# A language-model block on one core: the first layer's bias as a weight row, one of eight weight rows subtracted from the rest, two experts' low parts made by VectorE, and new orders on four engines

## The reference, cut to what matters

```python
# x is the layer-normalised hidden row: 4096 tokens x 64
gate_logits = x_flat @ Wg + bg + bias                       # 8 logits
topk_vals, topk_idx = jax.lax.top_k(gate_logits, 2)
topk_w = jax.nn.softmax(topk_vals, axis=-1)
h = jax.nn.relu(jnp.einsum('td,edh->teh', x_flat, W1) + b1) # 8 experts, 64 -> 128
y = jnp.einsum('teh,ehd->ted', h, W2) + b2                  # 128 -> 64
out = jnp.einsum('ted,te->td', y, combine)
```

## Time and profile before

| | us |
|---|---|
| median of 3 runs | 90.46 (89.78 to 91.33) |
| the profiled execution | 90.22 |
| its span, from the first to the last instruction | 88.4 |
| PE busy in the span | 76.5 (87%) |
| DVE busy | 73.0 (83%) |
| ACT busy | 69.1 (78%) |
| POOL busy | 57.2 (65%) |

### The profile page before, as it was taken

One profiled execution on the slowest core, in us unless ns is written; L12 is line 12 of the kernel. 1 busy time (PEld: TensorE's weight loads), 2 busy tenths in 40 slices (PEclk: granted clock), 3 DMA queues, 4 the chain that ended last, 5 costly groups with the idle time before them and its releaser, 6 DMA issues.

```text
span 88.4 us, 2799 instructions
## 1 busy us (share of the span) xinstructions
PE 76.5 (87%) x1004; PEld 48.7 (55%) x1004; DVE 73.0 (83%) x305; ACT 69.1 (78%) x141; POOL 57.2 (65%) x111
## 2 busy tenths in 40 slices
PE   0098899779869999999999999999999999999920
PEld 0055794444346676556556676654754557667900
DVE  5899989999994999699978999998995599349970
ACT  0579995428147998999999999999999987996530
POOL 7030009898718848599534889989897788983420
PEclk9999999995899999999999999999999999999998
...
GB/s 20 110 151 261 389 56 4 0 0 8 0 0 0 7 0 0 7 1 4 0 7 0 0 7 0 0 7 0 0 52 8 7 4 51 15 0 0 64 163 137
DMA packets 5919, 3.40 MB, mean 39 GB/s; under 512 B 4914, under 2 KB 5266, under 8 KB 5906
## 3 DMA queue, kind: packets, MB, share of 16 engines
...
q10 hardware_dynamic: 512, 0.31, 1.2%
...
...
## 4 chain that ended last, share of the span: by engine, by line
PE 47%; DVE 22%; ACT 14%; POOL 9%; issue 5%; POOLq 0%; ACTq 0%
PE bank L1344 12%; PE bank L1371 6%; PE bank L1353 6%; PE bank L1173 6%; ACT hid_lo L691 4%; PE bank L1368 3%; PE bank L1374 3%; ACT oneh_junk L631 2%; ACT hid_hi L684 2%; ACT ids_all L603 2%; POOL h_part L457 2%; PE bank L1257 2%; DVE prod_pair L1012 1%; DVE pT L925 1%; PE bank L1402 1%
## 5 line engine op out<-in xcount | busy, mean ns | idle before, releaser
L684 ACT ACTIVATE hid_hi<-bank,b_down 128x512 f16<-128x512 f32 (+1 forms) x40 | 26.5, 663 | 2.9 <-PE bank L1344 2.4
L691 ACT ACTIVATE hid_lo<-bank,b_col 128x512 f16<-128x512 f32 (+1 forms) x40 | 26.6, 664 | 0.1
L1353 PE MATMUL bank<-hid_hi,minus_h 128*128 128x512 f16 (+1 forms) x40 | 14.4, 361 | 0.2
L1344 PE MATMUL bank<-xT,w_hi 128*128 128x512 f16 (+1 forms) x40 | 14.4, 359 | 0.1
L1344 PE MATMUL bank<-xT,w_lo 128*128 128x512 f16 (+1 forms) x40 | 14.3, 357 | 0.0
L1006 DVE TENSOR_TENSOR prod<-bank,comb 128x512 f32<-128x512 f32 x14 | 9.4, 690 | 4.8 <-PE bank L1374 4.6
L559 POOL TENSOR_TENSOR half<-prod 128x256 f32<-128x256 f32 x12 | 8.8, 733 | 1.2 <-DVE prod L1006 0.4
L1173 PE MATMUL bank<-toe_hi,oneh_j 128*128 128x512 f16 (+3 forms) x24 | 9.0, 378 | 0.0
L1353 PEld LDWEIGHTS bank<-hid_hi,minus_h 128*128 128x128 f16 x40 | 3.9, 97 | 8.5 <-ACT hid_hi L684 6.6
L1173 PE MATMUL bank<-toe_lo,oneh_j 128*128 128x512 f16 (+3 forms) x24 | 8.5, 375 | 0.0
L1371 PE MATMUL bank<-w_lo,hid_hi 128*128 128x64 f16 x112 | 8.4, 193 | 0.0
...
## 6 DMA issues: line engine op xcount, KB each, us to landing
w_sb<-in_w1g_dram SPq DMA_DIRECT2D x1, 516.0 KB, 5.2
...
w_sb<-in_w2b_dram SPq DMA_DIRECT2D x1, 260.0 KB, 5.4
...
```

Of the source, the lines that this page charges most:

```text
L684: act.activation(hid_hi[:, k % 2, e, 0:m], bank[n % LBANKS][:, 0:m], ACT.Relu, bias=b1_down[:, e:e + 1], scale=KEEP * HSCALE / (XSCALE * X ...
L691: act.activation(hid_lo[:, k % 2, e, 0:m], bank[n % LBANKS][:, 0:m], ACT.Relu, bias=b1_col[:, e:e + 1], scale=HSCALE / (XSCALE * XSCALE)). ...
L1344: ins = mm(bank[n % LBANKS][:, 0:m], w[:, HID * e:HID * (e + 1)], xT[:, k % 2, 0:m], start=part == 0, stop=part == 1)
L1353: mm(bank[n % LBANKS][:, 0:m], minus_h[:], hid_hi[:, k % 2, e, 0:m], start=False, stop=True, skip_group_check=True).then_inc(s_rest, 1)
```

## The change

1. The first layer's bias becomes a row of its weights. The 64 entries of x sum to zero, so entry 63 is minus the sum of the others: the kernel subtracts weight row 63 from rows 0 to 62 (`w1_centre` on POOL, a 128x1032 subtraction, with a new 516 KB load `w63` ahead of `w2` on SP), and puts the bias into row 63. DVE sets entry 63 of x to a constant once (`bias_column`), and `rows_c` writes 63 entries of 64.
2. ACT no longer adds a bias in `high` and `low`, the scales become powers of two, and the two small activations that prepared the bias are gone. `w1_high` waits for `w1_centre`.
3. For experts 2 and 6 of every unit, PE's `take_high` and ACT's `low` are gone, and DVE writes `hid_lo` in one instruction: max(bank, 0) - `hid_hi` (`hidden_low`). These are ten of the forty. What waited for `s_hid` now waits for one of two semaphores.
4. The lists of calls of POOL, ACT, DVE and PE are new.

```diff
@@ the load (SP)
             sp.dma_start(w1_sb[:], w1g).then_inc(loads["w1"], 16)
-            sp.dma_start(w2_sb[:], w2b1).then_inc(loads["w2"], 16)
+            sp.dma_start(w63_sb[:], w63).then_inc(loads["w63"], 16)
+            sp.dma_start(w2_sb[:], w2).then_inc(loads["w2"], 16)
             sp.dma_start(b2_row[:], b2).then_inc(loads["b2"], 16)
@@ POOL
+            def w1_centre():
+                pool.wait_ge(loads["w1"], 16)
+                pool.wait_ge(loads["w63"], 16)
+                pool.tensor_tensor(w1_sb[:], w1_sb[:], w63_sb[:], ALU.subtract).then_inc(s_w1c, 1)
...
-            rsqrt_hidden(); table_values(); embed_parts(); skip_values(); rsqrt1(0); value_parts(); rsqrt2(0)
+            rsqrt_hidden(); bias_parts(); embed_parts(); w1_centre(); table_values(); skip_values(); rsqrt1(0)
...
@@ ACT
             def w1_high():
-                act.wait_ge(loads["w2"], 16)
-                act.mul(b1_col[:], w2_sb[:, EXPERTS * D:], HSCALE)
-                act.mul(b1_down[:], w2_sb[:, EXPERTS * D:], HSCALE * KEEP)
-                act.wait_ge(loads["w1"], 16)
-                act.mul(w1_hi[:], w1_sb[:], XSCALE).then_inc(s_w1h, 1)
+                act.wait_ge(s_w1c, 1)
+                act.mul(w1_hi[:], w1_sb[:], WS).then_inc(s_w1h, 1)
...
@@ DVE
+            def hidden_low(n):
+                k, e = n // EXPERTS, n % EXPERTS
+                m = P * SIZE[k]
+                dve.wait_ge(s_high, n + 1)
+                dve.scalar_tensor_tensor(hid_lo[:, k % 2, e, 0:m], bank[n % LBANKS][:, 0:m], 0.0, hid_hi[:, k % 2, e, 0:m],
+                                         ALU.max, ALU.subtract).then_inc(s_hidv, 1)
...
@@ PE, first_layer
                 else:
-                    pe_.wait_ge(s_hid, n + 1 - LBANKS)
+                    wait_expert(pe_, n - LBANKS)
...
-                if n:
+                if n and (n - 1) % EXPERTS not in DVE_LOW:
                     take_high(n - 1)
...
-            turn_ids(); spread_ids(0); spread_ids(1); spread_ids(2); spread_ids(3); turn_top(); fold_weights()
+            spread_ids(0); spread_ids(1); turn_ids(); spread_ids(2); spread_ids(3); turn_top(); fold_weights()
...
-            weights(0); turn_exps(); attend(0, 2); scores(0); scores(1); embed(0); weights(1); scores(2); attend(2, 4)
...
+            embed(0); weights(0); turn_exps(); scores(0); attend(0, 2); scores(1); weights(1); scores(2); embed(1)
...
```

More of the change, by code:

```diff
@@ L79, with build @@
 QW = C_PROJ + D + 2
-def build(nc, x, token_w, vecs, qkv, bias_table, w1g, w2b1, b2, out):
+def build(nc, x, token_w, vecs, qkv, bias_table, w1g, w63, w2, b2, out):
     ids_dram = nc.dram_tensor("ids_scratch", (SEQS, LEN), BF16, kind="Internal").ap()
@@ L370, in build, with by_dve, by_act, wait_expert @@
         LOGITS = bank[5][:, 448:448 + MAXB * EXPERTS]
+        DVE_LOW = (2, 6)
+        def by_dve(n):
+            return sum(i % EXPERTS in DVE_LOW for i in range(n))
+        def by_act(n):
+            return n - by_dve(n)
+        def wait_expert(eng, n):
+            if n % EXPERTS in DVE_LOW:
+                eng.wait_ge(s_hidv, by_dve(n + 1))
+            else:
+                eng.wait_ge(s_hid, by_act(n + 1))
         class Chain:
@@ L733, in _ @@
+            hidden(4, 1); choice_exp(4); hidden(4, 2); hidden(4, 3); hidden(4, 4); hidden(4, 5); hidden(4, 6)
+            hidden(4, 7); low(4, 7); read_look(0); read_look(1); read_look(2)
         @block.vector
@@ L1073, in _ @@
-            rows_b(0); rows_b2(0); part_low(0); rows_c(0); toeplitz_low(1); rows_d(0); skip_exps(); rows_a(1)
-            rows_b(1); rows_b2(1); key_part(1); choose_a(0); rows_c(1); key_part(2); rows_d(1); skip_key()
-            skip_key_rows(); choose_b(0); rows_a(2); choose_a(1); rows_b(2); rows_b2(2); choose_b(1); rows_c(2)
-            key_part(3); rows_a(3); rows_d(2); rows_b(3); rows_b2(3); weigh(0); weigh(1); choose_a(2); weigh(2)
-            rows_c(3); rows_a(4); choose_b(2); rows_d(3); weigh(3); rows_b(4); rows_b2(4); weigh(4); weigh(5)
@@ new lines, in _ @@
+            skip_masks(); skip_columns(); penalties(); values(); row_maxima(); split_exps(); toeplitz_low(1)
+            flat_weights(); w1_low(); rows_a(0); key_part(0); rows_b(0); rows_b2(0); part_low(0); rows_c(0)
+            key_part(1); rows_d(0); rows_a(1); skip_exps(); early_one_hots(); rows_b(1); rows_b2(1); skip_key()
+            rows_c(1); skip_key_rows(); choose_a(0); rows_d(1); hidden_low(2); key_part(2); choose_b(0); rows_a(2)
+            choose_a(1); rows_b(2); hidden_low(6); key_part(3); rows_b2(2); choose_b(1); rows_c(2); rows_a(3)
@@ new lines, in _ @@
+            hidden_low(10); rows_d(2); weigh(0); rows_b(3); rows_b2(3); weigh(1); hidden_low(14); choose_a(2)
+            rows_a(4); choose_b(2); weigh(2); rows_c(3); hidden_low(18); rows_b(4); weigh(3); rows_d(3); rows_b2(4)
+            hidden_low(22); weigh(4); weigh(5); rows_c(4); choose_a(3); rows_d(4); weigh(6); hidden_low(26)
+            choose_b(3); weigh(7); weigh(8); hidden_low(30); weigh(9); choose_a(4); weigh(10); choose_b(4)
+            hidden_low(34); weigh(11); weigh(12); weigh_pair(0); weigh(13); hidden_low(38); gather_two(); weigh_pair(1)
@@ L1435, in _ @@
-            turn(0); weights(2, 0, 1); weights(2, 1, 3); first_layer(0, 0); weights(2, 3, 4); embed(1)
-            first_layer(0, 1); scores(3); first_layer(0, 2); weights(2, 4, 5); first_layer(0, 3); skip_weights()
-            gate(0); weights(2, 5, 8); first_layer(0, 4); skip_scores(); first_layer(0, 5); weights(3, 0, 1)
-            weights(3, 1, 3); first_layer(0, 6); weights(3, 3, 5); turn(1); first_layer(0, 7); skip_turn()
-            attend(6, 4); first_layer(1, 0); gate(1); first_layer(1, 1); embed(2); first_layer(1, 2); weights(3, 5, 8)
@@ L1450, in _ @@
-            last_bias(3); last_bias(4); look_up(0); take_high(EXPERTS * UNITS - 1); last_layer(4); last_layer(5)
-            last_layer(6); last_layer(7); look_up(1); look_up(2)
+            embed(0); weights(0); turn_exps(); scores(0); attend(0, 2); scores(1); weights(1); scores(2); embed(1)
+            weights(2, 0, 1); attend(2, 4); weights(2, 1, 3); turn(0); weights(3, 0, 1); weights(3, 1, 3)
+            first_layer(0, 0); scores(3); weights(2, 3, 4); weights(2, 4, 5); first_layer(0, 1); gate(0)
@@ new lines, in _ @@
+            skip_weights(); skip_scores(); first_layer(0, 2); weights(2, 5, 8); first_layer(0, 3); skip_turn()
+            weights(3, 3, 5); weights(3, 5, 8); first_layer(0, 4); turn(1); attend(6, 4); first_layer(0, 5); gate(1)
+            first_layer(0, 6); first_layer(0, 7); embed(2); first_layer(1, 0); first_layer(1, 1); embed(3)
+            first_layer(1, 2); first_layer(1, 3); attend(10, 4); first_layer(1, 4); second_layer(0); first_layer(1, 5)
+            turn(2); first_layer(1, 6); first_layer(1, 7); second_layer(1); gate(2); embed(4); first_layer(2, 0)
@@ new lines, in _ @@
+            attend(14, 4); first_layer(2, 1); second_layer(2); first_layer(2, 2); first_layer(2, 3); second_layer(3)
+            first_layer(2, 4); first_layer(2, 5); second_layer(4); first_layer(2, 6); first_layer(2, 7); turn(3)
+            second_layer(5); first_layer(3, 0); last_bias(0); gate(3); first_layer(3, 1); second_layer(6)
+            first_layer(3, 2); second_layer(7); first_layer(3, 3); turn(4); first_layer(3, 4); first_layer(3, 5)
+            second_layer(8); first_layer(3, 6); first_layer(3, 7); second_layer(9); first_layer(4, 0); gate(4)
```

110 lines of the change are left out of this document (54 added, 56 removed).

## The result

Before 90.70 us (median of 4 runs, 89.78 to 91.33), after 94.69 (4 runs, 93.93 to 94.85): ratio 1.046, 95% interval 1.035 to 1.057. The change makes the kernel slower by some 4 us, by a late start, as forecast (93.6 was predicted). The profiled execution took 94.57, its span 92.8, against 90.22 and 88.4 before.

The account below looks back on a forecast made before the run. ACT was the tighter bound before; DVE's queue bounds afterwards. Start 24.4 plus 60.6 work plus 0.6 waits ends gather_two at 85.6 instead of 82.19, +3.4 on 90.22: 93.6 us, range 90.9 to 96.2.

Parts of the forecast that it names:

- b2's landing: At the start, b2 lands behind w63 and w2 at 12.2 us, between 10.2 and 13.6; POOL's bias_parts waits for it.
- Rival B: Start less late: b2 lands 1.4 us sooner, embed_parts is 1.2 shorter; no change, 91.0 us in all; chance 0.20.
- POOL agrees: At the start, POOL's queue behind w1_centre frees rsqrt1(0) at about 24.4 us, matching rows_a(0).
- the port: Shared SBUF port at the start: DVE's moved toe_lo holds POOL up to 0.7 us more, making the result 94.3.
- hid_lo on DVE: Ten new DVE instructions in the experts' stretch, 0.60 to 0.69 us each at full width, 5.7 us taken together.
- DVE's work in the stretch: From rows_a(0) to the end of gather_two, DVE has 54.2 + 5.7 + 1.3 - 0.6 = 60.6 us of work.
- rival C: Relief of ACT and PE pays and DVE's stretched operations shrink: faster, 86.4 or 88.5 us; chance 0.07.
- New waits: DVE's waits between rows_a(0) and the end of gather_two: 0.6 us, between 0 and the old 7.8.
- those for PE go: DVE's old waits for PE, 1.82 and 1.27 us, vanish because DVE itself is now later.
- the bias costs the same either way: On ACT, dropping the bias and changing the scales saves no time.
- The check on PE: first_layer(1, 1) on PE waits for hidden_low(6) on DVE; costs only where DVE has to wait in turn.
- rival D: DVE and PE wait for each other over banks holding low parts: 3 us more, 96.6 us; chance 0.11.

Follow-up runs that it names:

- experiment 8: experiment 1 with gather(10) and gather(11) ahead of the fin_parts on POOL, and look_up(0) behind last_layer(7) on PE: 94.22 us, ratio 1.038.
- 11: Changed kernel with b2 loaded first, w1_centre on DVE, the start orders of before, and gather(10) ahead of the fin_parts: 96.79 us, ratio 1.063.
- 4: Changed kernel with all forty low parts on PE and ACT, none on DVE: 96.44 us, ratio 1.068.
- 5: experiment 1 with all forty low parts on PE and ACT, none on DVE: 95.28 us, ratio 1.049.
- experiment 1: Changed kernel with the b2 load issued first, ahead of SP's wait for the ids: 92.59 us, ratio 1.025.
- 9: experiment 1 with the start of ACT, PE and DVE (up to toeplitz_low(0)) in the order of the kernel before: 92.98 us, ratio 1.022.
- experiment 7: Kernel before plus one 128x1032 POOL subtraction, into a tile nobody reads, where POOL was idle: 92.34 us, ratio 1.016.
- 6: experiment 1 with the w1_centre subtraction moved from POOL to DVE, behind toeplitz_low(0): 92.59 us, ratio 1.020.
- experiment 12: Changed kernel with b2 first, w1_centre on DVE, old start orders, embed(0) behind scores(1), attend(0) and squares(0) moved earlier: 93.43 us, ratio 1.028.

## Why the prediction was right

Right: the sign, and that the loss is a late start, made by POOL's queue behind `b2`. The sum's total was 1.0 us short (93.6 against 94.57 profiled; 94.69 in the median), within its own range: `gather_two` ended 0.5 later than predicted (86.10, not 85.6), and the end behind it, which I had left as it was, grew by 0.4. That it came so near is in part luck, since two pairs of errors cancelled. Step by step:

- **b2's landing**: predicted 12.2, at most 13.6; measured 13.4. `w63` added 1.3 us, as predicted (issued at 5.66, 6.0 to landing: 11.66, against `w1`'s 10.38). Most of the missing 1.2 is `w2`'s: it landed at 13.2, 1.6 behind `w63`, not 0.7; the loads were also issued 0.2 later. Rival B's other case, a small load overtaking, is refuted here: 2 KB issued at 6.61 came last. The Trainium skill (DMA: Bandwidth & Descriptors, "Queues, rings and completion order") allows an overtaking; this trace shows none.
- **bias_parts**: 2.0 predicted, 2.0 measured. **embed_parts**: 4.4 predicted, 3.0 measured, just under its lower end of 3.2: `w_lo`, beside which its first cast had taken 1.44, no longer ran beside it. **w1_centre**: 2.3 and 2.44. The errors cancel, which is luck, and `w_sb` is ready at 20.93, predicted 20.9 to 21.2.
- **rows_a(0)**: 24.4 and 24.48. But "POOL agrees", with `rsqrt1(0)` free at 24.4, was 1.1 too early: it started at 25.48, and DVE waited 0.43 for it (see the port, below).
- **hid_lo on DVE**: 0.60 to 0.69 predicted, 0.60 in a row and 0.69 alone measured; the ten are 6.3 us busy in records that overlap their neighbours by some 0.08 each, against 5.7 predicted in steps. No mistake there.
- **DVE's work in the stretch**: 60.6 predicted. Measured: 61.62 less 4.6 of waits behind the first mark, 57.0. This step was wrong by 3.6 us. Part of it is that `gate_bias` left the stretch (0.3 in steps), which I overlooked, and part that some of DVE's short operations shrank, which I had put under rival C only. POOL is 1.3 us less busy in the stretch; that this is the reason isn't shown. Two of them, from the groups of this stretch, the kernel before first:

```profile
L999 DVE TENSOR_TENSOR comb<-sel 128x32 f32<-128x32 f32 (+1 forms) x5 | 1.6, 319 | 0.2
```

```profile
L1029 DVE TENSOR_TENSOR comb<-sel 128x32 f32<-128x32 f32 (+1 forms) x5 | 1.2, 245 | 0.2
```

   Of the busy time, groups of this kind shrank by 2.0 us together (`gw`, `comb`, `xn`, `gd`, `var`), while `gs`, `xs` and `og` grew by 0.6. The rest of the 3.6 I can't place.
- **New waits**: 0.6 predicted, 4.6 measured ("under 2 us" was among my own signs). This step was wrong too, by 4.0, in the other direction. The old waits are nine, not ten; their sum of 7.8 is right. The claim "those for PE go" failed: 2.13 and 0.61 us at the end, behind POOL's `gather(10)` and `gather(11)`. The profile names PE's L1407 for the first, both before and after, and I took its word. But PE's block was there already (in experiment 8 the same `prod` ran 2 us sooner), and in both kernels the `prod` starts 0.1 us after `gather(10)` has left its buffer. For the kernel before:

```profile
76.54 0.32 POOL L561 TENSOR_TENSOR acc<-half 128x64 f32<-128x64 f32 x1
```

   and its `prod` at 76.96; after, the `acc` at 80.61 (0.32) and the `prod` at 81.03. Experiments 8 and 11 took the cause away, and this wait went. POOL comes later with the start, so a wait for it cannot be filled by a late DVE.
- So the forecast that DVE has no room left was wrong, and the sum held by luck: 3.6 us too much work and 4.0 us too few waits cancelled. By that sum, leaving the low parts off DVE (5.7 of work less, waits of at most the old 7.8) should have moved the time by -5.7 to +1.5; experiments 4 and 5 gave +1.8 and +2.2.
- **ACT**: "the bias costs the same either way" was wrong. An `hid_lo` of 128x512 in a row of them took a step of 0.57 before and takes 0.48 after, and with `hid_hi` that is part of the 11.5 us by which ACT is less busy. What this paid no run separates.
- **The check on PE**: `first_layer(1, 1)` did wait for `hidden_low(6)`, 0.9 us. PE's waits for `hid_lo` are 1.1 us in all, so rival D did not come about. **C**: refuted, as `rows_a(0)` was at 24.5; but half of it is true, since DVE had 57 us of work, near the 56 that I had named, and the low parts on DVE pay.
- **The port**: I expected DVE's `toe_lo` (0.68 us from 21.28) to hold POOL for up to 0.7, and the time to be 94.3 by it. That is what the trace shows: the two `vh` took 1.45 at 20.93, and 0.63 in experiment 1, where no such DVE operation lay beside them. What I had not seen is `w_lo` (1.20 from 22.74): under it the cast `vs_part` took 1.30, and 0.23 in experiment 1. These 1.9 us are why `rsqrt1(0)` came at 25.48. Without them it would have waited for `rows_a(0)` and started near 24.9 (an estimate: 0.42 behind that mark's start, as in experiment 1), so the two holds cost some 0.6 us, close to the 0.7 that I had named. And the port works the other way too: POOL's 2.44 us held DVE's `eg_part` to 2.72. DVE still waited 0.54 for `usq` afterwards, but `toe_lo`, queued behind it, thereby ran beside `table_values`.

What the 4.0 us consist of, as shown: 1.3 us, with 0.7 of tail, went when `b2` landed early (experiment 1); some 0.6 of the 1.3 is DVE holding POOL, which the early landing takes apart. Underneath lie causes that don't add: POOL's work under DVE's one-hots and its `w1_centre` (3.4 and 2.1 us of standing still in experiments 9 and 1, +1.4 alone in experiment 7), and orders of ACT and PE in which the late ids and `turn_exps` come later; what each order costs alone no run shows. Each of these is the next limit when the one before is taken away, which is why experiments 6 and 9 brought next to nothing. Against them stand the low parts, 1.8 to 2.2 us of gain. What stays open: which part of PE's new order keeps `rows_a(1)` at 28.5 in experiment 12, and whether an order exists in which the new layer wins.
